# Identity products on TensorE while the second and third layer norm make their statistics and between their transposes

## What is computed

```
x = x + cross_attention(layernorm(x), ctx, ctx)     # 16 heads of 16
x = x + state_space(layernorm(x))                   # projections, convolution over 4, scan over 64 steps, output
x = x + mixture(layernorm(x))                       # one shared expert, 12 routed, two per token
```

## Time and profile before

| | us |
|---|---|
| median of 3 runs | 1625.99 |
| lowest, highest | 1623.48, 1627.28 |
| the profiled execution, its own time | 1641.62 |
| its span, first to last instruction | 1639.9 |
| PE busy | 1363.9 (83%) |
| DVE busy | 1339.8 (82%) |
| ACT busy | 1055.8 (64%) |
| POOL busy | 996.3 (61%) |
| mean granted clock of PE | 0.963 |

### The profile page before, as it was taken

The page is one execution under the profiler, slowest core; times in us unless marked ns, Lnnn a source line. Parts: engine busy times, 40 slices in busy tenths (PEclk is TensorE's granted clock), DMA queues, the critical chain, the costliest instruction groups (busy, mean ns, idle before and its releaser), DMA issues. The chain is left out here.

```text
span 1639.9 us, 33488 instructions
## 1 busy us (share of the span) xinstructions
PE 1363.9 (83%) x12636; PEld 1028.4 (63%) x12636; DVE 1339.8 (82%) x1690; ACT 1055.8 (64%) x2454; POOL 996.3 (61%) x820
## 2 busy tenths in 40 slices
PE   5899999999999999878367667667666869999992
PEld 4788888888888888654133333333333748888882
DVE  4899999999999999956399999999998424666662
ACT  3666666666666665527399899899896224555550
POOL 1878888888888887637267667666665050333323
PEclk9999999999999999979699999999999789999996
DMA  4511111111111110037640300200000043888872
GB/s 118 184 43 40 43 40 42 42 42 41 42 42 42 42 42 8 2 54 191 103 80 1 44 1 1 45 1 1 1 1 1 1 157 120 301 299 309 310 274 87
DMA packets 105534, 132.83 MB, mean 81 GB/s; under 512 B 41022, under 2 KB 96645, under 8 KB 101932
## 3 DMA queue, kind: packets, MB, share of 16 engines
q1 hardware_dynamic: 92876, 59.83, 15.1%
q0 software_dynamic: 9312, 67.90, 11.6%
q10 hardware_dynamic: 3200, 3.15, 0.5%
HBM read 110.44 MB, written 14.45 MB: 76 GB/s over the span
## 5 line engine op out<-in xcount | busy, mean ns | idle before, releaser
L555 POOL TENSOR_TENSOR half<-prob 128x512 f32<-128x512 f32 (+1 forms) x208 | 266.6, 1282 | 108.9 <-ACT prob L591 107.3
L587 ACT ACTIVATE prob<-ps_s,mx 128x64 f32<-128x64 f32 (+1 forms) x624 | 152.0, 323 | 236.2 <-DVE prob L700 236.2
L1328 DVE TENSOR_TENSOR state<-ps_u,state 128x1024 f32<-128x1024 f32 x252 | 296.9, 1219 | 4.3
L695 DVE TENSOR_REDUCE mx<-ps_s 128x16 f32<-128x1024 f32 (+1 forms) x208 | 253.3, 1218 | 12.0 <-PE ps_s L628 8.3
L1287 PE MATMUL ps_y<-state,cz 128*32 128x256 f32 x2048 | 247.5, 384 | 2.1 <-DVE state L1328 1.1
L1214 ACT ACTIVATE ps_a<-A,dt 128x256 f32<-128x256 f32 x504 | 210.4, 463 | 45.2 <-DVE state L1323 45.2
L628 PE MATMUL ps_s<-qbd,kT 64*128 64x256 f32 (+1 forms) x1664 | 216.6, 395 | 21.2 <-ACT prob L587 15.6
L700 DVE TENSOR_TENSOR prob<-ps_s,mx 128x832 f32<-128x832 f32 (+1 forms) x208 | 213.1, 1024 | 7.1
L1269 PE MATMUL ps_u<-x_rows,b_diag 48*128 48x256 bf16 x1024 | 79.0, 274 | 163.2 <-DVE state L1328 134.9
L1198 POOL TENSOR_TENSOR state<-direct,state 128x1024 f32<-128x1024 f32 x64 | 151.8, 2371 | 94.4 <-PE ps_y L1287 94.3
L628 PEld LDWEIGHTS ps_s<-qbd,kT 64*128 64x128 f32 (+1 forms) x1664 | 150.4, 184 | 65.6 <-issue 29.6
(11 more groups left out here) (241 smaller groups left out, 3129.5 us busy)
## 6 DMA issues: line engine op xcount, KB each, us to landing
raw<-in_ctxT_dram SPq DMA_DIRECT2D x80, 268.0 KB, 2.8
x_rows<-ssm_x SPq DMA_DIRECT2D x96, 64.0 KB
raw<-in_ctxT_dram SPq DMA_DIRECT2D x16, 261.0 KB, 2.7
b_diag<-zeros SPq DMA_DIRECT2D x2, 2048.0 KB, 9.0
x_slots<-zeros SPq DMA_DIRECT2D x1, 3456.0 KB, 12.9
xg<-x_slots SPq DMA_DIRECT2D x27, 128.0 KB, 5.7
y_slots<-y SPq DMA_DIRECT2D x27, 128.0 KB
ssm_x<-xp ACTq DMA_DIRECT2D x8, 384.0 KB, 4.6
```

The lines of the kernel that those rows point to most:

```text
L555: pool.tensor_tensor(half[0:rows, :, :], prob[0:rows, g % SLOTS, :, 0:L // 2], prob[0:rows, g % SLOTS, :, L // 2:L], ALU.add).then_inc(hal ...
L695: nc.vector.tensor_reduce(mx[0:rows, g % 2, :], part, AX_X, ALU.max, negate=True)\
L1328: nc.vector.tensor_tensor(h, flat(ps_u[k % 2][:, :, :]), h, ALU.add).then_inc(state_ready, 1)
```

## The change

`layer_norm` gets a PSUM tensor of one bank that nothing reads, and PE writes products of the identity with itself into it: five that are 512 columns wide before it waits for the first normalised tile, and one of 128 columns behind the two transposes of each tile. The identity is float32. Nothing else waits for these products, and they wait for nothing. Both ln2 and ln3 get them.

```
+        unread = ctx.enter_context(nc.psum_tensor(f"{tag}_unread", [P, 512], F32))
...
         @block.tensor
         def _(pe):
+
+            def idle_product(copies):
+                nc.tensor.matmul(unread[:, 0:copies * P], sb["ident"][:, :],
+                                 sb["ident"][:, :].unsqueeze(1).broadcast_to([P, copies, P]), start=True, stop=True)
+
+            for _ in range(5):
+                idle_product(4)
             for t in range(TT):
                 pe.wait_ge(xln_ready, t + 1)
...
                 ins.then_inc(turned, 1)
+                idle_product(1)
```

## The result

The changed kernel takes 1619.86 us (median of 7 runs, 1619.07 to 1620.27) against 1626.79 (7 runs, 1623.48 to 1630.38) for the kernel before. The ratio is 0.9964 with a 95% interval of 0.9950 to 0.9978, so it is faster by 0.4%, 6.9 us by the medians, where 6.0 had been forecast. Two later series on other executions gave 0.9958 (0.9944 to 0.9972) and 0.9954 (0.9936 to 0.9972).

The account below looks back on a forecast made before the run. PE's clock, halved after idling in ln2 and ln3, was taken to slow work on the path to the end. Both norms' gains, 5.6 or 6.3 us, gave 6.0 off the median 1626.0: 1620.0 us, range 1615.5 to 1627.0.

Parts of the forecast that it names:

- 0.2 us gained by ACT's last copy: In each norm, the last transposed tile and ACT's last copy come some 0.2 us sooner at the full clock.
- The slower rival: Clock at 0.50 at the first transpose: tiles cost 0.92 us, both norms lose 3.7, 8.0 us lost, 1634.0; chance 0.12.
- the prediction's doubt about the identity's zeros: Point for the slower rival: the identity is nearly all zeros, so its products may not keep the clock; no separate size.
- for ln2 0.4 or 3.8 us: Behind ln2, dt and the first x product: 3.8 us gained if dt keeps the clock, 0.4 if it loses it.
- for ln3 5.2 or 2.5: Behind ln3, logits and first shared tile: 5.2 us gained if the logits keep the clock, 2.5 if they lose it.
- one stretch of narrow records keeping the clock and the other losing it: Main case, dt against logits: 5.6 us off if ln3 keeps it, 6.3 if ln2 does; 1620.0, chance 0.40.
- the forecast's own case in which ln2 keeps the clock and ln3 loses it: Half of the main case: 3.8 us from ln2 plus 2.5 from ln3, 6.3 us off.
- 4.9: Behind ln3: the count ends 4.9 us after the logits at full clock instead of 6.5, 1.6 us gained.
- both keep it: Rival: dt and the logits both keep the clock, 3.8 + 5.2 = 9.0 us off, 1617.0; chance 0.18.
- The rival that ln3's gain would stop at the long wait: PE's 12.90 us wait in the shared expert absorbs ln3's gain; ln2's 0.4 to 3.8 remains, about 1624.5; chance 0.16.

Follow-up runs that it names:

- 8-column variant: The changed kernel with all 26 added matmuls 8 columns wide instead of 512 or 128: 1632.04 us, ratio 1.0034 to the kernel before.
- filled: Changed kernel with six wide products before the first tile, none between tiles, one of 256 columns behind the last transpose: ratios 0.9957 and 0.9946 to the kernel before.
- spread variants: Filled, with dt matmuls among the first x product's: 1617.44 us, ratio 0.9949; then also five shared-expert gate records among the logits: 1614.00 us, ratio 0.9928.

## Why the prediction was right

**The price of the new work.** Forecast: five products in 4.4 us, ended 1.4 us before the first tile, a tile at 0.45 us, 0.2 us gained by ACT's last copy. Measured: 4.53 us, 1.31 us, 0.44 us, and from the last transpose's start to dt 0.99 instead of 1.14. All of it came out of rows of the kernel before.

**The clock through the norm.** Forecast to hold, from its staying at 1.00 for 3.4 idle us before and from the idle stretches being at most 1.5 us now. It held in every profile, in each norm that had the wide products. The slower rival (8.0 us lost if it did not) was real as a mechanism, but its price is not confirmed: that the 8-column variant lost 7.8 us in the two stretches is another sum. Its norms lost 2.2 us each and not 3.7, as a tile took 0.75 us, 2.4 came from dt and x, which ran at 0.50 nearly to their end, and 0.8 from the shared groups before the count. With the 128-column products and no wide ones, a tile at 0.50 took 0.86 us, near the 0.92 of the rival, but the clock came back before the last tiles. No run changed the data of the products, so the prediction's doubt about the identity's zeros is answered only as far as these products held the clock.

**What the better clock gives.** Forecast for ln2 0.4 or 3.8 us, for ln3 5.2 or 2.5, with one stretch of narrow records keeping the clock and the other losing it. The sum of 6.0 was near the 5.6 of the profile, but its terms were not those. In the first profile, and in the third (1.8 and 3.9), both dt and the logits kept the clock to their end, and it fell behind them, in the first x product and in the first shared groups: 1.8 us in ln2 and 3.8 in ln3. In the second it was 3.5 and 2.2, which is the forecast's own case in which ln2 keeps the clock and ln3 loses it (3.8 and 2.5). The term that was mis-sized is the fall: I had it within the narrow records or not at all, and it also comes behind them. In ln3, the count ended 6.1 us after the logits, not 4.9, since the first two groups of the shared tile ran at 1.2 GHz; only with the gate product among the logits was it 4.6. That the two errors met at the right sum is partly luck. The case "both keep it", 9.0 us, did not occur in the three profiles of the changed kernel; with the narrow records spread both keep it, and the stretches give 10.0 us, of which 1.9 are norms without products between the tiles: from the first transpose to dt or the logits it is 3.4 us there and 4.4 in the kernel before.

The reading of the page's clock row was loose at one place: counted from one, its dips stand at slices 18, 20, 32 and 33, and the one at 20 is PE's wait for the scan, not ln2. No term of the sum used it.

**The path.** Forecast that both gains reach the end. One norm alone gave 0.9977 and 0.9970, so both do. The rival that ln3's gain would stop at the long wait fell: on the chip with the wait, ln3 alone still gains 0.30%, as the wait moves with the scatter (56.8 us between the scatter and the routed tiles, 58.1 before; whether these 1.3 us are part of ln3's gain, one profile doesn't tell), and on the others there is no wait.

**The level of the time.** Taking the microseconds off the median, not a share of the profiled execution, was right: the profiled execution has the long wait, 18.1 us more than the profiles without it, and every run of the kernel before on the chip with the wait lies at 1638 to 1647 us, where its runs elsewhere lie at 1621 to 1630. That the 15.6 us between the two are the chip's follows from this; the first profile does not name its chip.

**Weight loads and transposes against the clock.** The 8-column variant's dt takes 6.96 us for 32 records at 0.50 and the changed kernel's 3.71 at 1.00, 0.22 and 0.12 us a record: weight loads follow the clock. The section "LDWEIGHTS (loading the stationary operand)" of "TensorE: Matmul & The Clock Gate" in the Trainium skill has one figure, the columns over 1.2. For 128 columns that is an estimate of 0.11 us; these runs agree with it at 1.00 and take twice as long at 0.50.

With wide products ahead of them, transposes alone held 1.00 (the second window of the variant with the wide products alone, and both norms of the filled and the spread variants). And in ln2 of the kernel before, the clock rose at 726.1 after nothing but transposes since 722.4; in its second profile and in ln3 alone it rose 0.5 us behind those transposes. That does not fit the Trainium skill, "TensorE: Matmul & The Clock Gate", section "Part 4: PE-mode transpose", by which the full clock doesn't engage for transposes. But the same 16 transposes in ln3 did not bring the clock back in any of the three profiles that have them there without products; it stayed at 0.50 through the logits. Why it rises in one place and not in the other was not tried.

## What to carry to other kernels

Read the granted clock beside every stretch in which PE is busy and somebody waits for it; where it is 0.50, ask what PE did just before. Idle wide matmuls in PE's waiting time cost nothing on the path; here they bought 0.3% for both norms by themselves, and with the products between the tiles 0.2 to 0.3% per norm, but check that they are wide: the same count of 8-column matmuls made the kernel 0.3% slower. What came out best is to mix records of few columns with wide ones that have to be done anyway, on top of the idle products; that gave 0.7% in all, against 0.4 to 0.5% for the idle work alone, with intervals that just overlap those of the changed kernel beside it. Whether the mixing needs the idle products in the norms was not run.

## What the runs showed of the hardware that had not been expected

A PE that is busy without a gap can still lose its clock: in three profiles of the changed kernel there are six stretches of 32 records of 8 or 12 columns, without a gap; in five of them the clock fell to 1.2 GHz, in the stretch or up to 1.1 us behind it. Sixteen transposes of 128 columns in 2.70 us, PE busy for nearly all of it, held it in ten stretches of five profiles, each with the last wide product at most 1.3 us before.

One chip has waits of ACT and DVE of up to 15 us in the shared expert, around the end of the scatter and the first gathers of the weights, in each of the four profiles taken there (56.8 to 58.1 us from the start of the scatter to the routed tiles); the first profile of the kernel before has it too, and the other nine have 39.9 to 40.0. What the engines wait for there is not in the trace, and was not tried.
